# A two-layer attention and expert kernel: preparation in chunks of two or four tiles, and setup in the block of attention

## The reference

```python
x = hidden
x = x + global_latent_attn(rmsnorm(x, norm1_w), ...)   # layer 0: causal, 16 heads of 8, keys and values shared by 4
x = x + local_gqa_attn(rmsnorm(x, norm2_w), ...)       # layer 1: the same shapes, each token sees the last 32
x = layernorm(hidden + x)
x = layernorm(x + shared_expert(x) + top-2 of 8 routed experts(x))
```

## Time and profile before

| | us |
|---|---|
| median of 3 runs (lowest, highest) | 778.27 (772.07, 780.87) |
| span of the profiled execution | 780.5 |
| first scores begin (slot 0) | 36.12 |
| first scores of tile 4 begin (slot 20) | 66.89 |
| the last tile of layer 0 is added | 536.85 |
| first scores of the last chunk begin | 571.98 |
| the last tile of attention is added | 592.07 |

### The profile page before, as it was taken

One profiled execution on the slowest core, in us unless ns is written; L12 is line 12 of the kernel. 1 busy time (PEld: TensorE's weight loads), 2 busy tenths in 40 slices (PEclk: granted clock), 3 DMA queues, 4 the chain that ended last, 5 costly groups with the idle time before them and its releaser, 6 DMA issues. The chain is left out here.

```text
span 780.5 us, 12122 instructions
## 1 busy us (share of the span) xinstructions
PE 630.5 (81%) x3926; PEld 341.8 (44%) x3926; DVE 506.6 (65%) x1325; ACT 431.2 (55%) x589; POOL 374.4 (48%) x419
## 2 busy tenths in 40 slices
PE   2478888888998886899999686987877799999950
PEld 1223332243543233444324242445766566666750
DVE  2577764477985477798448867657855567434864
ACT  4457867775765774466756444753442444444433
POOL 5356434445523443344233277651476056777831
PEclk9999989999999998899958897999889999999985
DMA  9136646000000000000000001010004023335151
GB/s 275 48 112 223 223 140 212 25 1 1 0 3 1 1 0 14 4 12 14 15 0 1 1 26 38 28 37 1 1 17 115 8 77 88 96 94 167 68 179 54
DMA packets 38125, 47.22 MB, mean 60 GB/s; under 512 B 8960, under 2 KB 35232, under 8 KB 37408
## 3 DMA queue, kind: packets, MB, share of 16 engines
q1 hardware_dynamic: 26976, 35.10, 14.8%
q0 software_dynamic: 4352, 9.05, 3.4%
q10 hardware_dynamic: 6736, 2.30, 1.1%
HBM read 35.29 MB, written 28.98 MB: 82 GB/s over the span
## 5 line engine op out<-in xcount | busy, mean ns | idle before, releaser
L875 ACT ACTIVATE prob<-ps_s 128x1024 f32<-128x1024 f32 x320 | 309.1, 1024 | 170.9 <-PE ps_s L1227 119.1
L1264 PE MATMUL ps_v<-prob,va 128*32 128x512 f32 x1152 | 170.6, 677 | 7.0 <-POOL prob L765 6.3
L1227 PE MATMUL ps_s<-qs,ks 32*128 32x512 f16 x576 | 107.6, 412 | 32.4 <-ACT prob L875 29.3
L1030 DVE STREAM_TRANSPOSE sums<-ps_v 128x512 f32<-128x512 f32 x62 | 44.3, 714 | 86.1 <-PE ps_v L1264 45.0
L765 POOL TENSOR_SCALAR_AFFINE_SELECT prob<-prob 128x1024 f32<-128x1024 f32 x64 | 70.3, 1116 | 53.8 <-ACT prob L875 53.5
L1497 POOL DMA_INDIRECT y_rows<-y,to_row x72 | 69.7, 968 | 42.4 <-DVE y L1618 24.1
L1227 PEld LDWEIGHTS ps_s<-qs,ks 32*128 32x128 f16 x576 | 25.4, 92 | 147.3 <-ACT prob L875 100.6
L1258 PE MATMUL ps_v<-prob,vd 128*128 128x256 f32 (+1 forms) x292 | 64.9, 374 | 12.1 <-DVE marked L1050 11.8
L1530 ACT ACTIVATE gated<-ps_gu 128x512 f32<-128x512 f32 x46 | 27.5, 597 | 80.6 <-PE ps_gu L1725 65.7
L1725 PE MATMUL ps_gu<-weights,rows_t 128*128 x144 | 68.9, 601 | 0.5 <-ACT rows_t L1535 0.5
L1258 PEld LDWEIGHTS ps_v<-prob,vd 128*128 128x128 f32 x292 | 53.4, 207 | 25.5 <-DVE prob L1057 14.7
(11 more groups left out here) (228 smaller groups left out, 1047.6 us busy)
## 6 DMA issues: line engine op xcount, KB each, us to landing
x_rows<-in_blank SPq DMA_DIRECT2D x8, 2112.0 KB, 9.2
rows<-x_rows SPq DMA_DIRECT2D x72, 66.0 KB, 2.1
chosen_y<-y_rows SPq DMA_DIRECT2D x8, 512.0 KB, 5.2
weights<-in_weights SPq DMA_DIRECT2D x1, 3456.0 KB, 13.3
out<-result ACTq DMA_DIRECT2D x8, 256.0 KB, 2.2
marked<-in_hidden SPq DMA_DIRECT2D x3, 512.0 KB, 5.5
r_in<-in_hidden SPq DMA_DIRECT2D x6, 256.0 KB, 2.9
y_rows<-y,to_row POOLq DMA_INDIRECT x72
```

Source lines behind the costliest of these rows:

```text
L875: act.activation(probs_at(n, 0, SLOT_COLS), scores_at(n, 0, SLOT_COLS), ACT.Exp, scale=HD ** -0.5 / GAIN ** 2).then_inc(exped, 1)
L1030: dve.transpose(sums[:].rearrange("p r b v -> p (r b v)"), sums_bank(q).rearrange("p r q -> p (r q)")).then_inc(sums_turned, 1)
L1227: last = pe.matmul(scores_at(n, j * BANK, BANK).rearrange("p (r q) -> p r q", r=REP), ks[b % QUERY_BATCHES][rows, kt * P:(kt + 1) * P], qs ...
L1264: last = pe.matmul(bank[g * VW:(g + 1) * VW, :, :], va[b % VALUE_BATCHES][:, kt, g, :], probs_at(n + g // 2, g % 2 * BANK, BANK).rearrange ...
```

## The change

The chunks get a length. `CHUNK_ORDER` now has (layer, batch, first tile, tiles), with 18 chunks: two of two tiles at the start (tiles 0 and 1, tiles 2 and 3 of batch 0) and two of two at the end (tiles 4 and 5, tiles 6 and 7 of batch 3 in layer 1). A chunk of two tiles follows `PREPARE_PAIR`, 27 steps with one projection and one turn of queries. `PAUSES` opens 6 steps before tile 2 and 8 before tile 4, and the gap before the last slots goes from 38 to 28 steps and now lies before tile 6. So steps after tile 4 have numbers that are 14 higher than before. The first scores' chunk starts 27 steps ahead of them instead of 37. Tiles 4 and 5 of the last batch have their slots before the gap (332 and 334), tiles 6 and 7 after it (364 and 365). `FILL` has new steps. The clearing of `vd1` moves from ACT to DVE, and the block of setup is dissolved into the block of attention.

```diff
+KEY_TURN = 2
 LOCAL_STEPS = 2
-LAST_LOCALS = 4
+LAST_LOCALS = 2
...
-PAUSES = {(1, 3, CT): 38}
-CHUNK_ORDER = [(0, 0, 0), (0, 0, 1), (0, 1, 0), (0, 1, 1), (1, 0, 0), (0, 2, 0), (1, 0, 1), (0, 2, 1),
-               (1, 1, 0), (0, 3, 0), (1, 1, 1), (0, 3, 1), (1, 2, 0), (1, 2, 1), (1, 3, 0), (1, 3, 1)]
+PAUSES = {(1, 3, TPB - 2): 28, (0, 0, 2): 6, (0, 0, CT): 8}
+CHUNK_ORDER = [(0, 0, 0, 2), (0, 0, 2, 2), (0, 0, 4, 4), (0, 1, 0, 4), (0, 1, 4, 4), (1, 0, 0, 4), (0, 2, 0, 4), (1, 0, 4, 4),
+               (0, 2, 4, 4), (1, 1, 0, 4), (0, 3, 0, 4), (1, 1, 4, 4), (0, 3, 4, 4), (1, 2, 0, 4), (1, 2, 4, 4), (1, 3, 0, 4),
+               (1, 3, 4, 2), (1, 3, 6, 2)]
...
-PREPARE_STEPS, PREPARE_VALUES = 36, 18
+PREPARE_PAIR = [(0, "square"), (2, "sum"), (3, "invert"), (4, "refine"), (5, "scale"), (7, "turn_tokens"), (8, "move_tokens"),
+                (9, "project", 0), (10, "rotate", 0), (12, "add"), (13, "turn_values"), (14, "move_values"), (14, "square_heads"),
+                (16, "sum_heads"), (17, "invert_heads"), (18, "normalise"), (19, "split_heads"), (21, "pair_parts"),
+                (23, "turn_parts", 2), (24, "move_parts", 2), (24, "spread_keys"), (25, "turn_parts", 0), (26, "move_parts", 0)]
+PREPARES = {CT: PREPARE, 2: PREPARE_PAIR}
+PREPARE_STEPS, PREPARE_VALUES = {CT: 36, 2: 27}, {CT: 18, 2: 14}
...
-SPACING = 14
-FIRST_STARTS = (-37, -16)
-CLEAR_VALUES_AT, CLEAR_BLOCKS_AT = {-33: 1, -32: 2}, {-31: 0, -15: 1}
-ONES_AT, BLOCK_ONES_AT = {-20: 1, -18: 2}, {-6: 0, -4: 1}
-BAND_AT, REPEAT_BAND_AT = -36, -31
+SPACING = {CT: 14, 2: 11}
+FIRST_STARTS = (-27, -16, -4)
+CLEAR_VALUES_AT, CLEAR_KEYS_AT, CLEAR_BLOCKS_AT = {-23: 1, -22: 2}, {-21: 0, -9: 1}, {-19: 0}
+ONES_AT, BLOCK_ONES_AT = {-14: 1, -13: 2}, {2: 0, 14: 1}
+BAND_AT, REPEAT_BAND_AT = -20, -12
...
-FILL = [(6, "fill_gate", 0), (7, "fill_gated", 0), (12, "fill_hidden", 0), (15, "fill_gate", 1), (16, "fill_gated", 1),
+FILL = [(5, "fill_gate", 0), (5, "fill_gated", 0), (8, "fill_hidden", 0), (10, "fill_gate", 1), (11, "fill_gated", 1),
...
+        step += PAUSES.get((0, b, qt), 0)
         start, inside = step, list(LOCAL_INSIDE.get((b, qt), []))
...
         def _(sp):
+            sp.dma_start(x[:, 0:2, :], st["hidden_tiles"][:, 0:2, :]).then_inc(st["x_loaded"][0], 16)
+            sp.dma_start(st["down_t"][:], ins["g_kv_down_t"]).then_inc(st["latent_loaded"], 16)
+            sp.dma_start(st["up"][:], ins["g_kv_up"]).then_inc(st["latent_loaded"], 16)
+            sp.dma_start(x[:, 2:CT, :], st["hidden_tiles"][:, 2:CT, :]).then_inc(st["x_rest"][0], 16)
+            sp.dma_start(x[:, CT:TPB, :], st["hidden_tiles"][:, CT:TPB, :]).then_inc(st["x_rest"][1], 16)
+            for to, of in (
...
+            dve.memset(vd[1][:], 0.0).then_inc(later_blocks_zeroed, 1)
...
-                for t in range(CT):
+                if not k:
+                    pe.wait_ge(made, MADE)
+                for t in range(chunk[3]):
                     last = pe.transpose(side_tokens(chunk)[:, t * P:(t + 1) * P], xn[:, t, :], ident[:])
...
                     pe.wait_ge(st["global_loaded"], 16 * GLOBAL_LOADS)
+                    pe.wait_ge(folded, 2)
...
                     if layer:
                         pe.wait_ge(values_out, GROUPS * (local_number[chunk] + 1))
                     else:
-                        pe.wait_ge(rope, rope_value(chunk_number[chunk], 1, "values"))
-                if q == QTILES - LAST_LOCALS:
-                    pe.wait_ge(fill_moves, FILLS)
+                        pe.wait_ge(rope, roped_value(chunk_number[chunk], "values"))
                 if w == firsts[q] and bank_of[q] >= 2:
                     take_side(bank_of[q] - 2, added, q + 1)
                 elif w == firsts[q] and before[q] is not None:
...
+            for m in ("ident", "ident_half"):
+                pool.affine_select(out=st[m][:], in_=st[m][:], compare_op=ALU.not_equal, fill=1.0, base=0,
+                                   pattern=[[-1, P]], channel_multiplier=1).then_inc(made, 1)
+            pool.wait_ge(made, MADE)
             at_every_step(attend, {"square": square, "scale": scale, "add": add, "square_heads": square_heads,
                                            "pair_parts": pair_parts, "spread_keys": spread_keys,
                                    "route_power": route_power, "send": send, "fill_hidden": fill_hidden,
...
+                    (st["cos"][0][:], ins["cos_g"].rearrange("(t p) d -> p t d", p=P)),
+                    (st["sin"][0][:], ins["sin_g"].rearrange("(t p) d -> p t d", p=P)), (st["wo"][0][:], ins["g_wo"])):
+                act.dma_start(to, of).then_inc(st["global_loaded"], 16)
             nc.scalar.preload_act_table_set("natural_log_exp_and_others")
+            act.wait_ge(made, MADE)
             at_every_step(attend, {"invert": invert, "invert_heads": invert_heads, "route_move": route_move,
                                    "choose_exp": choose_exp, "fill_gated": fill_gated, "fill_moved": fill_moved})
...
 
+            pe.wait_ge(st["latent_loaded"], 32)
+            pe.matmul(latent_product, st["down_t"][:], st["up"][:], start=True, stop=True).then_inc(folded, 1)
```

More of the change, by code:

```diff
@@ L130 @@
 BAND_STEPS = 17
+MADE = 6
 FILLED = {0: (1, 0), 1: (1, 1), 3: (2, 0)}
@@ L402, in stages_beside @@
         for chunk, start in zip(CHUNK_ORDER, starts):
-            for when, *stage in PREPARE:
+            for when, *stage in PREPARES[chunk[3]]:
                 if stage[0] in ("turn_values", "move_values", "spread_keys") and not chunk[0]:
@@ L437, in attention_layers @@
     for chunk, start in zip(CHUNK_ORDER, starts):
-        needed = min(slot_step[n] for n, (q, _, _) in enumerate(slots) if tiles[q][:2] == chunk[:2] and tiles[q][2] // CT == chunk[2])
-        assert start + PREPARE_STEPS <= needed, (chunk, start, needed)
+        needed = min(slot_step[n] for n, (q, _, _) in enumerate(slots)
+                     if tiles[q][:2] == chunk[:2] and chunk[2] <= tiles[q][2] < chunk[2] + chunk[3])
+        assert start + PREPARE_STEPS[chunk[3]] <= needed, (chunk, start, needed)
     route_starts = []
-    for k, (_, b, c) in enumerate(ROUTED):
-        start = max(ROUTE_AT[k], added_step[position[1, b, c * CT + CT - 1]] + 1)
+    for k, (_, b, first, count) in enumerate(ROUTED):
+        start = max(ROUTE_AT[k], added_step[position[1, b, first + count - 1]] + 1)
         while banks_of(starts, route_starts + [start]) is None:
@@ L659, in square @@
             def square(chunk, k):
-                layer, b, c = chunk
+                layer, b, first, count = chunk
                 if layer:
-                    pool.wait_ge(added, position[0, b, c * CT + CT - 1] + 1)
-                elif b == 0 and c:
-                    pool.wait_ge(st["x_second"], 16)
+                    pool.wait_ge(added, position[0, b, first + count - 1] + 1)
+                elif b == 0 and first:
+                    pool.wait_ge(st["x_rest"][first // CT], 16)
                 else:
@@ L1005, in split_heads @@
                 dve.wait_ge(norm, norm_value(k, "normed"))
-                after(dve, turned, TURNS * k)
-                dve.tensor_copy(by_head[:, :, 0, :], heads(sqh[:])).then_inc(split, 1)
+                after(dve, turned, turns_before(k))
+                to, of = by_head(chunk), heads(of_rows(sqh, chunk))
+                dve.tensor_copy(to[:, :, 0, :], of).then_inc(split, 1)
                 dve.wait_ge(split, SPLITS * k + 1)
-                dve.tensor_tensor(by_head[:, :, 1, :], heads(sqh[:]), by_head[:, :, 0, :], ALU.subtract
-                                  ).then_inc(split, 1)
+                dve.tensor_tensor(to[:, :, 1, :], of, to[:, :, 0, :], ALU.subtract).then_inc(split, 1)
             def move_parts(chunk, k, j):
-                layer, b, c = chunk
+                layer, b, tile, count = chunk
                 dve.wait_ge(turned, turn_value(k, j))
@@ L1074, in route_add @@
             def route_add(chunk, k):
-                _, b, c = chunk
-                dve.wait_ge(added, position[1, b, c * CT + CT - 1] + 1)
+                _, b, first, count = chunk
+                dve.wait_ge(added, position[1, b, first + count - 1] + 1)
                 dve.wait_ge(r_loaded, 16 * (k + 1))
@@ L1167, in turn_parts @@
                 take_side(bank_for[chunk, "turn_parts", j], parts_out, turn_value(k, j))
-                if j == TURNS - 1:
-                    for t in range(CT):
+                if j == KEY_TURN:
+                    for t in range(chunk[3]):
                         last = pe.transpose(side_keys(chunk)[:, t * P:(t + 1) * P],
@@ L1242, in weigh @@
                     pe.wait_ge(exped, n + 2)
-                if qt % CT == 0 and (kt == qt or layer):
-                    chunk = (layer, b, qt // CT)
+                chunk = chunk_at.get((layer, b, qt))
+                if chunk and (kt == qt or layer):
                     if layer:
```

241 lines of the change are left out of this document (117 added, 124 removed).

## The result

| | us |
|---|---|
| before, median of 20 runs (lowest, highest) | 775.84 (771.41, 781.91) |
| after, median of 20 runs (lowest, highest) | 784.68 (776.89, 790.75) |
| ratio of after to before, 95% interval | 1.009 (1.0063 to 1.0117) |

The kernel became some 7 us slower by the ratio, and 8.8 by the medians. That one was run beside the first experiments, with the ratio 1.0089 (1.0054 to 1.0124).

The account below looks back on a forecast made before the run. PE, busy 81% of the span, was taken to set the cost in the long middle, and chains of waiting instructions at both ends. Terms 3 + 3 + 3.7 - 7.7 = +2.0 on 780.5 gave 782.5, less 2.2 forecast 780, range 766 to 790.

Parts of the forecast that it names:

- The 2.2 us that I took off: Whole kernel: the median of runs lies 2.2 us below the profiled span, so 782.5 became a forecast of 780.
- First scores: Start of attention: the shorter first chunk and merged setup bring the first scores from 36.12 to 25.6, -10.5 us.
- rival (c): Start: setup in the same block brings nothing, 2.6 us less gained on the first scores; no chance of its own.
- Slot 6: Tile 2's first scores: at about 45.5, where they came at 46.11; the 10.5 us are given back, 0 us.
- Slot 20: Tile 4's first scores: from 66.89 to 71.5, +4.6 us, bounds -1.7 and +9.4.
- Start in sum: Start up to tile 4, with 1.5 us off for the next chunks being further on: +3 us, from -3 to +8.
- The middle: Long stretch before the gap: half the old last chunk is prepared there, +3 us of PE, bounds 0 and 5.
- T: Addition of the last tile of layer 0, formerly at 536.85; forecast to come 6 us later.
- The pause: From T to the last chunk's scores: from 35.1 to 38.8 us, +3.7, from -1 to +8; `move_tokens` at T + 19.8.
- Behind the scores: Last chunk's scores to the end of attention: 20.4 us becomes 12.7, -7.7, bounds -9 and -5; POOL finishes last.
- Rival (b): Start: PE stays at lower speed, slot 20 at 79 or later (decided after 77), 788 in all; chance 0.24.
- Rival (a): Short chunks pay: slot 20 at 65.2, middle's work in PE's idle time, shorter pause; -15 us, 763; chance 0.21.

Follow-up runs that it names:

- the first experiments: The changed kernel timed again, beside kernels with only the merged setup and DVE clearing, that plus start pairs, that plus end pairs; ratios 1.0089, 0.9933, 1.0082, 0.9989.
- `merge`: Against the kernel before: only setup in the block of attention and `vd1` cleared on DVE, all chunks four tiles; 771.25 us, ratio 0.9933.
- `third_earlier`: The changed kernel with the third chunk (tiles 4 to 7 of batch 0) six steps earlier, pauses kept; ratio 1.0083 to the kernel before.
- `merge_pause`: `merge` plus the pause of 8 steps ahead of tile 4, with nothing to prepare in it; 786.83 us, ratio 1.0141 to the kernel before.
- `short_pauses`: The changed kernel with pauses of 2 and 1 steps, not 6 and 8, second and third chunks 3 and 9 steps earlier, routing moved; 772.88 us, ratio 0.9966 to before.
- `both_fixed`: `short_pauses` with the first Silu moved behind the exponential of `choose` on ACT; 770.18 us, ratio 0.9937 to the kernel before.
- `end_fixed`: `merge` plus pairs at the end of layer 1, with the first Silu behind the exponential of `choose` on ACT; 771.59 us, ratio 0.9942 to the kernel before.

## Why the prediction came out right, and where it did not

The forecast was 780 with a range of 766 to 790 and the likeliest case "within 1%". The measured 784.68 and the ratio 1.009 lie inside, at the slower end. The sum was +2.0; by the ratio it should have been +7. The 2.2 us that I took off compare a span with device times, which are about 1.7 to 2.1 us above the span of the same execution in all later runs. So the execution behind the rows of before was some 4 us above its median of three, and I worked from slow rows.

- **First scores**, 25.6: 25.41, right. DVE's clearing took 3.47 us and ended at 5.19, so the first sum, due at 4.22, began 0.9 us late; I had the clearing done by 4.5.
- **The merged setup** I counted only as 2.6 us of the first scores, to be given back like the rest, and rival (c) held it to be worth nothing. It is worth 5 us (`merge`), together with the clearing on DVE. That hides how bad the start became: against `merge` the pairs and their pauses cost 12.
- **Slot 6**, 45.5: 42.60 by its exponential. The weighings of tiles 0 and 1 took 3.63 us for 24, not 5.8. That the lead of the first scores is given back was right: it comes 3.5 us ahead of before, and the lead was 10.7.
- **Slot 20**, 71.5: 72.90, near, by two errors that cancel. The second projection was 3.5 us earlier than my 44, and the stretch behind it 32.4 us long and not 27.5. **This is the step that failed.** I interpolated between two rows and took fewer slots in the stretch for a shorter stretch. What sets slot 20 is PE's order: a pause in slots does not only give time to preparation, it puts every step of other tiles and chunks that falls into it ahead of the next scores, with their waits. `third_earlier` and `merge_pause` show it at that place, `short_pauses` that it is most of the loss. That 71.5 came near is luck: nothing ties the two errors together, and in the four profiles that share this order slot 20 lies anywhere between 70.91 and 74.71.
- **Start in sum**, +3: +5.6 up to 250 us. Of the 1.5 us that I took off for the further progress of the next chunks, 0.4 are there (6.0 at slot 20).
- **The middle**, +3: from 5.6 to 7.1 at T, 1.5. Such a number is uncertain by several us, since `merge` and before drift apart by 8.5 us between 340 us and T with the same steps, all of it by 430 us. In that part the execution of before had the lower clock for longer: from 400 to 420 us its granted clock is 0.57, with PE busy for 18.96 of 20 us, and that of `merge` is 0.99.
- **The pause**, +3.7 (the heading's 3.8 is a slip): +5.9. `move_tokens` at T + 19.3 (I had 19.8) and seven table loads (seven) came as worked out. From there to the scores it was 21.7 and not 19.0. The Trainium skill (ScalarE: Activation LUTs, What ACT_TABLE_LOAD costs) adds a drain to each load. Here too the trace disagrees: the function behind the load at 559.29 starts 1.30 us after it.
- **Behind the scores**, -7.7: from the scores to the start of the last addition 12.1 us instead of 20.1, so -8.0. POOL is the last to finish, as I said, with a send at 598.38, but it does not set the last addition, which waits for PE (the same wait of 0.41 as before).
- **Rival (b)**, PE slow at the start: its sign came true and its rows too (granted clock 0.58 to 0.74 from 56 to 86). It is a part of the loss, up to 4 us ahead of slot 20 by the four profiles of the same order, but not the main one: its point of decision, slot 20 after 77, was not reached, and `both_fixed` has slot 20 at 65.59 with a clock nearly as low ahead of it. What the low clock behind slot 20 costs was not measured alone. **Rival (a)** needed slot 20 at 65.2. `short_pauses` has it at 65.56 and gains 3 us on before, not 15.

**The best version** that was run is `merge`, with `both_fixed` and `end_fixed` no different within the intervals (0.9933, 0.9937, 0.9942). The simplest of the three is enough: dissolve the setup block, clear `vd1` on DVE and leave the chunks as they are. Which part of `merge` brings its 5 us was not tested.

## What to carry to other kernels

When every engine runs in a written order, an inserted pause is not free time. List what the order lets in ahead of the next important instruction, and price the waits of those rows, on the engine that they hold up. A shorter chain to the first result is worth nothing if the same engines must then finish other work before the second. And time each part of a change of several parts alone, for here a gain of 5 us and a loss of 12 stood in one kernel.
